# The output bias of an attention layer: as a product in TensorE's bank, or as an addition on GpSimd

## The reference

```
attn = softmax(mask(q k^T * SCALE)) + 1e-9       # 16 heads of 16, window of 128 keys back
A    = (attn v) @ Wo.T + bo                      # q, k, v = xn @ W.T + b; bo is one row of 256
F    = top-2 of 8 experts(xn), weighted, + one shared expert(xn)
out  = x + A + F
```

## Time and profile before

| | |
|---|---|
| runs | 1717.61, 1720.82, 1721.35 us; median 1720.82 |
| span of the profiled execution, first to last instruction | 1707.4 us |
| its own time beside the span | not given by the page; the median of the runs is 13.4 us above the span |
| busy share PE, PEld, DVE, ACT, POOL | 90%, 74%, 65%, 58%, 65% |
| mean granted clock of TensorE | 0.963 of full speed |
| POOL L1473 (bias additions) | 32, 41.2 us busy |
| POOL L1479 (additions of routed rows) | 64, 82.7 us busy |

### The profile page before, as it was taken

How to read it: one execution, slowest core, us unless ns; L and a number is a source line. 1 busy time by engine, 2 the same in 40 slices (tenths; PEclk the granted TensorE clock), 3 DMA queues, 4 the chain that set the end, 5 groups by cost and what they waited for, 6 DMA issues and landing times.

```text
span 1707.4 us, 38917 instructions
## 1 busy us (share of the span) xinstructions
PE 1539.4 (90%) x11382; PEld 1267.9 (74%) x11382; DVE 1106.2 (65%) x3788; ACT 985.4 (58%) x2043; POOL 1105.5 (65%) x1158
## 2 busy tenths in 40 slices
PE   4888869999999999999998898888998989888897
PEld 4677748999998888889996566666766666666665
DVE  7898866666666666666667566666666666666642
ACT  5677745455545455544554566666666665666663
POOL 1877774443334443334432689989888888988888
PEclk9899989999999999999996799999999999999999
DMA  6777755555555555555655677676777676667642
GB/s 189 260 267 254 272 198 187 159 173 162 163 160 160 159 167 164 162 159 160 187 184 134 149 167 158 129 157 157 164 152 175 151 168 153 149 137 156 163 121 82
DMA packets 228581, 288.89 MB, mean 169 GB/s; under 512 B 59488, under 2 KB 146144, under 8 KB 228512
## 3 DMA queue, kind: packets, MB, share of 16 engines
q1 hardware_dynamic: 170064, 207.30, 44.2%
q10 hardware_dynamic: 45488, 45.36, 9.3%
q0 software_dynamic: 12960, 35.41, 8.3%
HBM read 198.07 MB, written 79.95 MB: 163 GB/s over the span
## 4 chain that ended last, share of the span: by engine, by line
PE 43%; POOL 30%; issue 15%; DVE 8%; ACT 2%; ACTq 1%; POOLq 1%; DMA 1%; DVEq 0%
PE psum L152 25%; PE psum L961 11%; POOL plain_arena L1441 5%; POOL plain_arena L1439 5%; POOL plain_arena L1466 4%; POOL plain_arena L1479 3%; POOL split_arena L1458 3%; POOL plain_arena L1473 2%; POOL plain_arena L408 2%; PE psum L1518 2%; PE psum L1148 2%; POOL plain_arena L411 2%; PE psum L1560 1%; POOL split_arena L1453 1%; POOL plain_arena L1449 1%
## 5 line engine op out<-in xcount | busy, mean ns | idle before, releaser
L152 PE MATMUL psum<-split_arena 128*128 128x512 f32 (+2 forms) x4752 | 946.4, 352 | 11.5 <-DVE split_arena L1252 4.2
L152 PEld LDWEIGHTS psum<-split_arena 128*128 128x128 f32 x4752 | 757.5, 194 | 133.9 <-issue 24.9
L1791 DVE CUSTOM_DVE_ANT_0 plain_arena<-psum,mask 128x256 f32<-128x256 f32 (+1 forms) x1024 | 338.6, 385 | 234.9 <-PE psum L1518 214.6
L1675 ACT ACTIVATE plain_arena<-psum 128x512 f32<-128x512 f32 (+1 forms) x512 | 250.3, 542 | 231.4 <-PE psum L1541 188.2
L1111 POOL TENSOR_TENSOR split_arena<-plain_arena,split_arena 128x1024 fp32r<-128x1024 f32 x43 | 103.3, 2402 | 228.1 <-ACT split_arena L1183 227.8
L1217 ACT ACTIVATE plain_arena<-psum 128x512 f32<-128x512 f32 (+1 forms) x172 | 90.2, 524 | 250.2 <-PE psum L152 218.5
L961 PE MATMUL psum<-split_arena 128*128 128x256 f32 x1704 | 218.1, 286 | 3.5 <-DVE split_arena L1282 3.5
L961 PEld LDWEIGHTS psum<-split_arena 128*128 128x128 f32 x1704 | 208.1, 191 | 5.8 <-DVE split_arena L1282 4.1
L1287 DVE TENSOR_TENSOR plain_arena<-psum,plain_arena 128x512 f32<-128x512 f32 (+1 forms) x172 | 102.5, 596 | 140.0 <-ACT plain_arena L1217 90.3
L1103 POOL DMA_INDIRECT plain_arena<-xn_d,run_ix x142 | 136.7, 963 | 69.4 <-POOL run_ix L1100 35.2
L1439 POOL TENSOR_SCALAR_AFFINE_SELECT plain_arena<-plain_arena 128x1024 f32<-128x1024 f32 x128 | 140.4, 1097 | 36.6 <-ACT plain_arena L1675 35.7
(11 more groups left out here) (199 smaller groups left out, 1890.8 us busy)
## 6 DMA issues: line engine op xcount, KB each, us to landing
plain_arena<-in_gate_w SPq DMA_DIRECT2D x43, 512.0 KB, 3.4
plain_arena<-in_up_w SPq DMA_DIRECT2D x43, 512.0 KB
plain_arena<-in_down_w SPq DMA_DIRECT2D x43, 512.0 KB
plain_arena<-in_x SPq DMA_DIRECT2D x32, 512.0 KB, 6.9
q_d<-split_arena SPq DMA_DIRECT2D x32, 512.0 KB, 3.2
k_d<-split_arena SPq DMA_DIRECT2D x32, 512.0 KB, 4.9
split_arena<-q_d SPq DMA_DIRECT2D x128, 128.0 KB, 3.7
split_arena<-k_d SPq DMA_DIRECT2D x128, 128.0 KB, 3.9
```

The costliest lines, as they stand in the source:

```text
L152: last = pe.matmul(out, lhs_t(p), rhs(q), start=(begins and c == 0 and k == 0), stop=(ends and c == len(chunks) - 1 and k == 2), skip_grou ...
L1675: act.activation(b_pt[:, g % 2, 2 * p + par, 4 * half:4 * half + n, :].rearrange("p k s -> p (k s)"), psum[:, 2 + par, 0:n * P], ACT.Exp, ...
L1791: last = dve.tensor_tensor_reduce(b_junk[:, 2 * par + i % 2, 0:cols], psum[:, par, at:at + cols], mask[:, 2 * P - cols:2 * P], -1.0, 3e38, ...
```

## The change

add_bias disappears from POOL, and b_f counts four additions for a sequence. add_routed of the first of two routed rows now waits for the load of x itself. On PE, a product over all 128 rows of the array opens each projection bank: its stationary operand is a 128x128 tile of ones, its moving operand a tile bias_rows of 128 rows by 512 columns. Row 0 of that tile is the high part of the bias (rounded to the format of the products) twice side by side, row 1 the low part, all other rows are zero, so that the sum over the rows is the bias in every row of the bank. The hidden products then add to it. The tile is made once, before turn 0: ACT copies the bias to its rounded form after its sigmoid, DVE subtracts, keeps row 1 of the difference with column 1 of the identity, and joins row 0 of the rounded form to it in two halves; POOL fills the ones. DVE does its part before its first masked_max.

```diff
@@ tiles, semaphores
+        bias_hi = sb("bias_hi", [P, D], F32R)
+        bias_lo = sb("bias_lo", [P, D], F32)
+        bias_rows = sb("bias_rows", [P, 2 * D], F32R)
+        all_ones = sb("all_ones", [P, P], F32R)
...
+        b_bhi = sem("b_bias_hi")
+        b_bias = sem("b_bias_rows")
+        b_one = sem("b_all_ones")
@@ b_gpsimd
-                    pool.wait_ge(b_f, 6 * b) if not is_first(b) else None
+                    pool.wait_ge(b_f, 4 * b) if not is_first(b) else None
...
-            def add_bias(b, half):
-                v = b_o[:, 2 * half:2 * half + 2, :]
-                pool.wait_ge(b_ldo, 16 * b + 16)
-                pool.tensor_tensor(v, v, bo_sb[:, :].unsqueeze(1).to_broadcast([P, 2, D]), ALU.add).then_inc(b_f, 1)
-
             def add_routed(b, half, n):
                 v = b_o[:, 2 * half:2 * half + 2, :]
                 pool.wait_ge(b_sc, 8 * b + 4 * half + 4)
-                pool.wait_ge(b_f, 6 * b + (half + 1 if n == 0 else 2 * half + 3))
+                if n == 0:
+                    pool.wait_ge(b_ldo, 16 * b + 16)
+                else:
+                    pool.wait_ge(b_f, 4 * b + 2 * half + 1)
...
-                    if h in (12, 14) and valid(t - 1):
-                        add_bias(t - 1, (h - 12) // 2)
...
+            pool.memset(all_ones[:, :].bitcast(F32), 1.0).then_inc(b_one, 1)
@@ b_tensor, project_hidden
+                if m == 0 and a % 2 == 0:
+                    if is_first(b) and a == 0:
+                        pe.wait_ge(b_bias, 4)
+                        pe.wait_ge(b_one, 1)
+                    pe.matmul(psum[:, 7 - a // 2, :], all_ones[:, :], bias_rows[:, :], start=True, stop=False,
+                              skip_group_check=True)
...
-                               begins=(m == 0 and a % 2 == 0), ends=False)
+                               begins=False, ends=False)
@@ b_scalar, before its turns
+            act.copy(bias_hi[:, :], bo_sb[:, :]).then_inc(b_bhi, 1)
@@ b_vector, finish
-                dve.wait_ge(b_f, 6 * b + 2 * half + 4)
+                dve.wait_ge(b_f, 4 * b + 2 * half + 2)
@@ b_vector, before its turns
+            dve.wait_ge(b_bhi, 1)
+            dve.tensor_tensor(bias_lo[:, :], bo_sb[:, :], bias_hi[:, :].bitcast(F32), ALU.subtract).then_inc(b_bias, 1)
+            dve.wait_ge(b_bias, 1)
+            dve.tensor_scalar(bias_lo[:, :], bias_lo[:, :], ident[:, 1:2], None, ALU.mult).then_inc(b_bias, 1)
+            dve.wait_ge(b_bias, 2)
+            for n in range(2):
+                dve.scalar_tensor_tensor(out=bias_rows[:, n * D:(n + 1) * D], in0=bias_hi[:, :].bitcast(F32),
+                                         scalar=ident[:, 0:1], in1=bias_lo[:, :], op0=ALU.mult, op1=ALU.add
+                                         ).then_inc(b_bias, 1)
```

## The result

| | before | after |
|---|---|---|
| median of six runs, us | 1721.09 (1717.61 to 1722.62) | 1726.14 (1723.99 to 1729.61) |
| ratio, 95% interval | 1 | 1.0033 [1.0021, 1.0045] |
| span and time of the profiled execution, us | 1707.4, time not given | 1722.3, 1723.99 |
| POOL busy, us | 1105.5 | 1067.8 |
| PE busy, us | 1539.4 | 1552.3 |

The changed kernel is 5.7 us slower by the ratio, 3.6 to 7.7 by its interval; forecast were 4.5. POOL lost 38 us of work and the time did not notice.

The account below looks back on a forecast made before the run. A cycle of hand-overs among POOL, PE and ACT was taken as the bound. Additions 0, products 0, preparation +4.2, cold start +0.7, end -0.4 gave +4.5 us, 1725.3 us; range 1719 to 1730.5.

Parts of the forecast that it names:

- The cycle: Steady attention turn: hand-overs among POOL, PE and ACT close on themselves and set turns of 46.89 or 48.49 us.
- the additions at 0: POOL's 32 bias additions, 41 us busy, only become waiting before step 15's hidden_lo: gain 0, bounds 0 and 41.
- The 32 products at 0: PE's added bias products in steps 0 and 1 hide in its stands: 0 per turn, bounds 0 and 0.55.
- the stand that was named: PE's 0.79 us wait before step 1's transposed scores, expected to hide the first product and shrink to 0.51.
- The price of one: One 128x512 bias product on PE, taken as 0.28 us; 32 would cost 9 us if nothing hid them.
- Preparation +4.2: Start of attention: DVE's first masked maximum comes 4.2 us later behind the bias-row work; bounds 0 and 4.6.
- Cold start +0.7: First ten score products run at TensorE's half clock after PE's longer stand: +0.7 us, bounds 0 and 1.5.
- Rival 1: First two turns: a later stand absorbs the start delay, -0.4 to +0.7 us, 1720.9 us; chance 0.14.
- End -0.4: Kernel's end: removed additions on the chain gain 0.4 of 2.5 us, as ACT's copy is late; bounds -1.0 and +0.1.
- Rival 3: Steps 0 to 2: fuller PE stops the clock falls after step 6's stand, -8.3 us to 1712.5; chance 0.06.
- the 13.4 us: Gap between profiled span 1707.4 and median 1720.82, added to the predicted span 1711.9 to give 1725.3.

Follow-up runs that it names:

- e4: Kernel before with POOL's bias additions taken out and nothing in their place (output lacks the bias): ratio 1.0003 [0.9993, 1.0013].
- e5: Changed kernel with the preparation on POOL and each bias product issued twice: ratio 0.9994 [0.9982, 1.0007] against the kernel before.
- e11: Kernel before with hidden_hi and rows_hi earlier in ACT's list and PE's step 6 projection ahead of its values products: ratio 0.9736.
- e3: Changed kernel with the preparation of the bias rows moved to POOL, behind its last memset: ratio 1.0008 [0.9999, 1.0017] against the kernel before.
- e2: Kernel before with only the preparation of the bias rows added (ACT's copy, DVE's four instructions): ratio 1.0035 [1.0019, 1.0051].
- both traces of the kernel before: The first profile (span 1707.4 us) and a rerun of the kernel before without edit (span 1722.6 us, ratio 1.0003).
- e12: Changed kernel with only ACT's copy of the bias moved to the start of its expert stage: ratio 1.0015 [1.0005, 1.0025] against the kernel before.
- e6: Changed kernel with preparation on POOL and PE's step 6 projection ahead of that step's values products: ratio 0.9939 against the kernel before.

## Why the prediction was right, point by point

- *The cycle, and the additions at 0.* Right, and shown by e4. The proof in the traces of before and after is the wait of hidden_lo at step 15, 2.00 to 4.53 us where 4.5 was forecast, and 32.8 us more waiting there over 13 turns.
- *The 32 products at 0.* Right. The first went into the stand that was named, 0.79 to 0.55. For the second I allowed 0.1 to 0.2 us of lateness; none over 0.03 is seen. e5 shows that even twice as many are free, within its interval (-3.1 to +1.2 us). The price of one was too high in the sum that used it as a bound: 0.28 was taken, 0.24 came off the stand.
- *Preparation +4.2.* Measured by DVE's two starts 4.92 - 0.61 = 4.3 us. The sum had the right order of events; the multiplication, of which no row showed the form, took 0.35 where 0.3 was taken.
- *Cold start +0.7.* The first values products came 5.0 to 5.3 us later, so 0.7 to 1.0 are left for it. Rival 1, a delay that is absorbed, falls with it. That an earlier fall of the clock costs time there can be read from the traces in which DVE starts at once. Counted from DVE's last copy, the clock falls 5.1 us on in e11, 4.6 in the first trace of before, 3.1 in the second and 2.3 in e3; from the first masked maximum to the first values products they take 26.36, 26.53, 26.82 and 26.88 us. In after and e2 PE goes on 5.6 us after the copy, with the clock at half already, and the same stretch is 27.48 and 27.45. So the direction is shown and the size fits; that all of the last 0.6 us is the clock's is argued. A window of after, 1 us of the first score products:

```profile
919.00:920.00 1.00, 1.00 (x4) 0.72 (x4) 0.52 (x3) 0.00 (x0) 0.00 (x0) 0.50 1.04 168
```

- *End -0.4.* Half right. In e3 and e4 the stretch from the last values products to the end is 0.3 us shorter than in both traces of the kernel before (27.8 against 28.1). In after it is 28.3, so the term came out at +0.2 there. What was late next there is not only ACT's copy: after hidden_lo and one addition, POOL waits for a DMA that it used to find landed.

```profile
1706.35 1.29 POOL L1465 TENSOR_TENSOR split_arena<-plain_arena,split_arena 128x512 fp32r<-128x512 f32 x1 [2.09 <-ACT split_arena L1721]
1707.60 1.30 POOL L1484 TENSOR_TENSOR plain_arena<-plain_arena 128x512 f32<-128x512 f32 x1
1709.44 1.30 POOL L1456 TENSOR_TENSOR plain_arena<-plain_arena 128x512 f32<-128x512 f32 x1 [0.54 <-DMA plain_arena<-rz_d]
```

  I had not looked for the reciprocals' landing when I moved normalise forward. In e3 and e4 the same instruction has no such wait, so there the 0.3 us is kept; in e12 the stretch is 28.0.

- *Rival 3, the clock.* Of the 14 groups at step 6 seven run at half in both traces of before, seven in after and seven in e5; the products at steps 0 and 1 do not touch it, e6 shows that work in the right place ends it. There the Trainium skill ("TensorE: Matmul & The Clock Gate", Part 1, "What's actually happening"), which has activity release the throttle, and the trace agree: no group at half in e6, where PE works in what was its stand.
- *What was off:* the profiled execution was taken as a plain one. Of the 13.4 us between its span and the median only 1.7 are what a timed run has beyond its span; the rest is a shorter execution, mostly ahead of the attention stage, perhaps of another chip. The sum used only differences inside the attention stage, so nothing came of it.

## What to carry to other kernels

Work taken from POOL was worth nothing here because no late wait of another engine ended on it: follow one period round until it closes, and ask of the removed instruction whether the next wait on its own engine is ended by somebody else. Constants that a change needs must be made where the engine is idle; put on the first instruction of a stage, behind another engine's last one, five small instructions cost more than 41 us of removed work gave. And the same closed cycle names the edit that pays: here one copy, moved ahead in its engine's list, was worth 36 to 41 us.

## What the runs showed of the hardware

- TensorE's clock falls to half in seven of 14 turns although PE is busy 90% of a turn, always at one place, after a stand of 1.67 us that itself follows one of 0.9, and each fall costs 1.6 us. With the stand cut to 0.43 us no step-6 group runs at half (e6).
- Two traces of the same kernel can differ by 13 us before they reach a stage in which they are 2.1 us apart (802.9 and 805.0): compare stages between marks, not spans. The kernel before took 1711.15 us on one chip and 1720.5 and 1720.88 on two others.
- A 128x512 product of this number format, between others, lengthens PE's list by 0.23 to 0.24 us at the full clock (after and e5).
